# Narrow products for unit 1 as well, and one ScalarE copy for both groups of a half, in a fused embedding, interaction and MLP kernel

## The reference

```python
e = jnp.stack([tbl_f[ids[:, f]] for f in range(32)], axis=1)      # (512, 32, 64)
def layer(X, prev, W, b):
    x = jnp.einsum('bmd,bhd->bmhd', X, prev).reshape(bsz, m * h, d)
    return jnp.einsum('oc,bcd->bod', W, x) + b[None, :, None]
x1 = layer(e, e, W0, b0)          # 128 outputs
x2 = layer(e, x1, W1, b1)         # 128 outputs
z = concat([x1.sum(2), x2.sum(2)], 1)
h = relu(concat([z, dense_ctx], 1) @ W_top1 + b_top1)   # 272 -> 512
h = relu(h @ W_top2 + b_top2)                           # 512 -> 256
y = h @ W_top3                                          # 256 -> 1
```

## Time and profile before

| what | value |
|---|---|
| time, median of 3 runs | 196.35 us (196.08 to 196.5) |
| profiled execution, span from first to last instruction | 194.2 us |
| median less span | 2.15 us |
| TensorE matmul busy | 181.0 us, 93% |
| ScalarE busy | 144.9 us, 75% |
| VectorE busy | 137.3 us, 71% |
| GpSimd busy | 123.8 us, 64% |
| mean granted TensorE clock | 0.991 |

### The profile page before, as it was taken

How to read it: one execution, slowest core, us unless ns; L and a number is a source line. 1 busy time by engine, 2 the same in 40 slices (tenths; PEclk the granted TensorE clock), 3 DMA queues, 4 the chain that set the end, 5 groups by cost and what they waited for, 6 DMA issues and landing times.

```text
span 194.2 us, 8803 instructions
## 1 busy us (share of the span) xinstructions
PE 181.0 (93%) x3815; PEld 157.7 (81%) x3815; DVE 137.3 (71%) x307; ACT 144.9 (75%) x349; POOL 123.8 (64%) x134
## 2 busy tenths in 40 slices
PE   6999999869669959999999999989999999999985
PEld 6999999749557738878898877868888879889984
DVE  2007799994499999999996499977765796693100
ACT  2499977549848997899868879979677797776333
POOL 3777787877777777777777777777777777000000
PEclk9999999999999997999999999999999999999999
DMA  6991111111123334427211411331141114010100
GB/s 182 311 339 33 27 29 24 29 25 30 27 51 64 84 83 75 118 54 177 50 30 30 81 30 30 50 58 30 32 83 32 30 32 75 17 23 14 29 3 0
DMA packets 16520, 12.26 MB, mean 63 GB/s; under 512 B 12513, under 2 KB 12897, under 8 KB 16482
## 3 DMA queue, kind: packets, MB, share of 16 engines
q1 hardware_dynamic: 12242, 7.44, 15.1%
q0 software_dynamic: 4096, 4.20, 11.2%
q10 hardware_dynamic: 144, 0.07, 0.1%
HBM read 9.59 MB, written 0.00 MB: 49 GB/s over the span
## 4 chain that ended last, share of the span: by engine, by line
POOL 47%; PE 31%; issue 16%; DMA 3%; ACT 2%; DVE 0%; ACTq 0%
POOL rows L626 47%; PE psum L458 13%; PE psum L220 7%; PE psum L545 3%; PE psum L527 3%; DMA rows<-table,idx 2%; PE psum L480 2%; PE psum L516 2%; PE psum L190 1%; DMA t_sb<-ids 1%; ACT t_sb L261 1%; PE psum L562 1%; DVE acc_sb L465 0%; ACT acc_sb L731 0%; ACT xx L271 0%
## 5 line engine op out<-in xcount | busy, mean ns | idle before, releaser
L626 POOL DMA_INDIRECT rows<-table,idx x128 | 123.1, 962 | 40.8 <-issue 38.7
L288 DVE TENSOR_TENSOR prod<-psum,xx 128x256 f32<-128x256 f32 (+3 forms) x160 | 85.7, 603 | 22.2 <-ACT xx L271 12.0
L261 ACT ACTIVATE t_sb<-psum 64x308 f32<-64x308 f32 (+1 forms) x180 | 76.4, 425 | 10.2 <-PE psum L205 3.9
L458 PE MATMUL psum<-coef,t_sb 128*64 128x128 f32 (+1 forms) x954 | 53.7, 275 | 0.0
L458 PEld LDWEIGHTS psum<-coef,t_sb 128*64 128x64 f32 (+1 forms) x954 | 47.4, 131 | 4.3 <-issue 4.1
L220 PE MATMUL psum<-prod,xx 64*32 64x154 f32 x1920 | 42.4, 300 | 2.0 <-ACT coef L731 0.9
L257 DVE COPY t_sb<-psum 64x308 f32<-64x308 f32 x64 | 30.8, 481 | 10.8 <-PE psum L220 9.5
L220 PEld LDWEIGHTS psum<-prod,xx 64*32 64x32 f32 x1920 | 30.7, 107 | 9.4 <-issue 5.9
L271 ACT ACTIVATE xx<-psum 128x256 f32<-128x256 f32 x32 | 12.3, 386 | 11.0 <-PE psum L190 10.6
L190 PE MATMUL psum<-ident,rows 128*128 128x128 f32 x64 | 13.6, 295 | 3.1 <-DVE prod L288 2.0
L358 DVE TENSOR_TENSOR t_sb<-t_sb,coef 128x64 f32<-128x64 f32 (+8 forms) x63 | 15.8, 321 | 0.2
(11 more groups left out here) (39 smaller groups left out, 120.9 us busy)
## 6 DMA issues: line engine op xcount, KB each, us to landing
rows<-table,idx POOLq DMA_INDIRECT x128, 2.7
t_sb<-t_sb SPq DMA_DIRECT2D x28, 64.0 KB
w_sb<-w1t SPq DMA_DIRECT2D x3, 512.0 KB, 6.9
t_sb<-w0x SPq DMA_DIRECT2D x1, 768.0 KB, 10.3
w0g_sb<-w0g SPq DMA_DIRECT2D x1, 512.0 KB, 9.2
w_sb<-top SPq DMA_DIRECT2D x2, 256.0 KB
w_sb<-top SPq DMA_DIRECT2D x1, 512.0 KB
w_sb<-w1t SPq DMA_DIRECT2D x1, 384.0 KB, 4.7
```

Of the source, the lines that this page charges most:

```text
L261: copy_t(act, lambda o, i: act.activation(o, i, ACT.Copy), 0, u, v)
L288: return dve.tensor_tensor(at(p, col, out), at(psum, XT[g] * BANK + a, first), at(x, x0 + b, second), ALU.mult)
L458: return pe.matmul(bank(ACC, half * O, O, j, width), t_sb[:, c:c + width], w, start=i < places, stop=i >= n - places, tile_position=(0, j))
L626: pool.indirect_dma_start(rows[:, c:c + D], None, table[:, :], bass.IndirectOffsetOnAxis(ap=idx[:, g:g + 1], axis=0))\
```

## The change

`NARROW` becomes 2, so unit 1 is in narrow form too, and its groups come, with unit 0's, before the coefficient transposes; the row transposes of unit 2's second half lie between the two. `COPIER` alternates between ScalarE and VectorE over the 14 groups. VectorE's products of unit 1's second half move from after the folds to before the far folds. From unit 2 on, VectorE copies p = 1 of the second group as before, and ScalarE copies p = 1 of the first group with two instructions of 64 x 308 and p = 0 of both groups with two instructions of 64 x 616. In unit 15's first half ScalarE copies all four parts with four of the latter form, in its second half ScalarE and VectorE take one p each. For this a half's 16 rows lie differently in T, and `ids` is transposed to match. TensorE waits for copies once for each wide half, for all groups before it.

```diff
-NARROW = 1
+NARROW = 2
...
-        COPIER = [int(n >= 5 and n % 3 == 2) for n in range(V_GROUPS)]
+        COPIER = [n % 2 for n in range(V_GROUPS)]
...
-        def copier(group, p):
-            return int(p == 1 and (group % 2 == 1 if 8 <= group < 4 * (ALL - 1) else group < 8 or group % 4 > 1))
+        BOTH, FIRST_GROUP, SECOND_GROUP = (0, 2), (0, 1), (1, 1)
+        LAST_HALF = 2 * ALL - 1
+
+        def copier(half, n):
+
+            if half < 2 * NARROW or half == LAST_HALF - 1:
+                return [(0, BOTH), (1, BOTH)] if n == 0 else []
+            if half == LAST_HALF:
+                return [(n, BOTH)]
+            return [(1, FIRST_GROUP), (0, BOTH)] if n == 0 else [(1, SECOND_GROUP)]
...
-            for n in range(2):
-                wait(pe, t_copied[n], copied(n, 4 * u + v - 1))
+            for n in range(2 if u < NARROW or v % 2 == 0 else 0):
+                wait(pe, t_copied[n], copied(n, 4 * u + v - (1 if u < NARROW else 0)))
...
+        def wide_copy(eng, copy, n, u, g):
+
+            mine = copier(2 * u + g, n)
+            if not mine:
+                return
+            if u == UNITS and g == 0:
+                eng.wait_ge(coef_tr, V_GROUPS)
+            if u >= 2 * UNITS:
+                eng.wait_ge(block_done, (u - 2 * UNITS) // 2 + 1)
+            for p, (t, groups) in mine:
+                eng.wait_ge(t_done, 4 * u + 2 * g + t + groups)
+                for e in range(2):
+                    src = at(psum, (TG + 2 * t) * BANK + e * COLS, [[1, COLS], [BANK, 2 * groups], [2 * COLS, 2]], D * p, D)
+                    dst = at(t_sb, t_at(u) + g * SUB + GROUP * p + 4 * t, [[CHUNK, COLS], [2, 2 * groups], [1, 2]], D * e, D)
+                    last = copy(dst, src)
+            last.then_inc(t_copied[n], 1)
...
-            for v in range(4):
-                t_group(pe, 0, v)
+            for u in range(NARROW):
+                t_half(pe, u, 0)
+                t_half(pe, u, 1)
+            transpose_rows(pe, 2, 1)
             for n in range(V_GROUPS):
...
-                if n == 10:
-                    transpose_rows(pe, 2, 1)
...
-            t_half(pe, 1, 0)
-            t_half(pe, 1, 1)
...
+            for u in range(NARROW):
+                copies(u, 0)
+                copies(u, 1)
+                fields_in(2, u)
             for n in range(V_GROUPS):
                 if COPIER[n] == 0:
                     copy_coef(act, plain, n)
-                if n == 10:
-                    act_xx(act, 2, 0)
-                    act_gram(act, 2, 0)
...
-            act_xx(act, 2, 1)
-            copies(1, 0)
-            act_gram(act, 2, 1)
-            copies(1, 1)
...
             products(dve, 1, 0)
+            products(dve, 1, 1)
             copied_w(dve, 2)
...
-            products(dve, 1, 1)
...
-            for v in range(4):
-                dve_copy_t(dve, 1, v)
             products(dve, 2, 0)
...
-        a["ids"][NARROW * UNIT:].reshape(-1, TILES // 2, 2, 2, 2, M).transpose(2, 4, 5, 0, 1, 3).reshape(128, -1)], axis=1)
+        a["ids"][NARROW * UNIT:].reshape(-1, 2, 2, 2, 2, 2, M).transpose(2, 5, 6, 0, 1, 3, 4).reshape(128, -1)], axis=1)
```

More of the change, by code:

```diff
@@ L175, in t_at @@
             return u // UNITS % 2 * COLS * CHUNK + u % UNITS * UNIT
-        def copier(group, p):
-            return int(p == 1 and (group % 2 == 1 if 8 <= group < 4 * (ALL - 1) else group < 8 or group % 4 > 1))
+        BOTH, FIRST_GROUP, SECOND_GROUP = (0, 2), (0, 1), (1, 1)
[6 more added lines that the diff above has]
+            return [(1, FIRST_GROUP), (0, BOTH)] if n == 0 else [(1, SECOND_GROUP)]
         def copied(n, groups):
-            return sum(copier(i, p) == n if i // 4 >= NARROW else p == n == 0 for i in range(groups) for p in range(2))
+            halves = sum(copier(h, n) != [] for h in range(2 * NARROW, groups // 2))
+            return (min(groups, 4 * NARROW) if n == 0 else 0) + halves
         def transpose_rows(pe, u, g):
@@ L245, in copy_t, with act_copy_t, dve_copy_t @@
                 eng.wait_ge(block_done, (u - 2 * UNITS) // 2 + 1)
-            eng.wait_ge(t_done, 4 * u + v + 1)
-            if u < NARROW:
[L248 to L264, removed]
+            for p, (t, groups) in mine:
[5 more added lines that the diff above has]
+            last.then_inc(t_copied[n], 1)
+        def act_copy_t(act, u, g):
+            if u < NARROW:
+                narrow_copy(act, u, 2 * g)
+                narrow_copy(act, u, 2 * g + 1)
+            else:
+                wide_copy(act, lambda o, i: act.activation(o, i, ACT.Copy), 0, u, g)
+        def dve_copy_t(dve, u, g):
+            wide_copy(dve, dve.tensor_copy, 1, u, g)
         def act_xx(act, u, g):
@@ L746, in _, with copies, fields_in @@
                 copy_cross(act, n)
-            for g in range(2):
-                act_copy_t(act, 0, 2 * g)
-                act_copy_t(act, 0, 2 * g + 1)
+            def copies(u, g):
+                act_copy_t(act, u, g)
+            def fields_in(u, g):
+                act_xx(act, u, g)
+                act_gram(act, u, g)
+            for u in range(NARROW):
+                copies(u, 0)
+                copies(u, 1)
+                fields_in(2, u)
             for n in range(V_GROUPS):
@@ L886, in _ @@
                 for g in range(2):
-                    dve_copy_t(dve, u, 2 * g + 1)
+                    dve_copy_t(dve, u, g)
                     products(dve, u + 1, g)
             copy_acc(dve, dve.tensor_copy, 7)
-            dve_copy_t(dve, ALL - 1, 2)
-            dve_copy_t(dve, ALL - 1, 3)
+            dve_copy_t(dve, ALL - 1, 0)
+            dve_copy_t(dve, ALL - 1, 1)
             copy_acc(dve, dve.tensor_copy, 8)
```

15 lines of the change are left out of this document (6 added, 9 removed).

## The result

The change made the kernel slower: 199.48 us in the median of 6 runs (197.98 to 200.09) against 196.48 for the kernel before (6 runs, 196.08 to 198.08), a ratio of 1.0142 with a 95% interval of 1.0107 to 1.0176. The forecast was 196.05 with a range of 195.5 to 196.65. The profiled execution took 198.76 us and spans 196.9, 2.7 more than before's 194.2.

What follows compares the result with a forecast made beforehand. GpSimd's row gathers were taken to bound the kernel up to the border near 128 us, TensorE after it. Setup gain 0, merged copies 0.31 us: 194.2 - 0.31 = 193.9, plus 2.15 gives 196.05 us, range 195.5 to 196.65.

Steps and rivals of the forecast that it cites:

- The border: Unit 11's second half, 128.09 us: TensorE waits 0.92 us for gathered rows; only gains after 133 us move the end.
- The setup's sum: First narrow matmuls to first contraction: 16.8 us against 18.07, with one idle gap of 1.52 us kept (bounds 0 to 3.0).
- The conclusion from the bounds: Setup 2.8 us earlier to 0.2 later lies inside TensorE's 0.92 us border wait, so its gain at the end is 0.
- The coarser wait: Wide halves wait for all copies of the half before: hidden by gather wait before 128 us, 0.2 us to spare behind.
- The merged copies: ScalarE's copies take 2.23 us a half, 0.38 less; sum of block 5 at 157.02 us starts 0.31 us earlier.
- The last half's copies: Unit 15's second half: VectorE's two copies take 1.58 us; packing up to 0.25 us later, cost taken as 0.
- What lies around the span: Time outside the profiled span, 2.15 us (median 196.35 against span 194.2), added to the forecast span.
- the merge saves nothing: Rival: merged copies take 0.87 us each, unit 11's first half starts 0.2 us late; 196.55 us, chance 0.06.
- the gathers move: Rival: moved folds shift VectorE-GpSimd meetings; 196.65 us if later (chance 0.13), 195.45 if earlier (0.19 together with rows sooner).
- the setup's gain passes through: Rival: the border is no floor, so 1.3 + 0.31 us less; 194.75 us, chance 0.06.
- rows land sooner: Rival: gathered rows land 0.3 us sooner at the border; 195.75 us, chance 0.19 together with gathers earlier.
- The clock rival: Rival: longer waits for rows drop the clock at 128 us, 1.0 us more; 197.05 us, chance 0.04.

Runs made afterwards that it cites:

- The spread kernels: Kernels with unit 1's narrow groups dealt between the coefficient transposes (e3, e5, e7, e9, e12); ratios to the kernel before 0.9978 to 1.0007.
- e7: e3 with two already satisfied waits in front of the second wide group of every half; ratio to the kernel before 1.0007.
- e9: e3 with 28 already satisfied waits in the setup, before unit 0's narrow groups; ratio to the kernel before 0.9985.
- e11: Changed kernel with the copies, waits and ids of the kernel before for units 2 to 11, merged copies from unit 12 on; ratio to the kernel before 1.0042.
- e5: e1 with unit 1's narrow groups dealt between the coefficient transposes, copies of the kernel before; ratio to the kernel before 0.9978.
- e1: Kernel before with the new setup order alone, old wide copies and waits; median 197.66 us, 0.44% slower than the kernel before.
- e13: e2 with unit 1 copied in the small pieces of the kernel before, merged copies from unit 2 on; ratio to the kernel before 1.0023.
- e12: e3 with merged copies from unit 12 on only; ratio to the kernel before 0.9988.
- e2: Changed kernel with the setup of the kernel before (unit 1 wide, behind the coefficient transposes); 198.81 us.
- e3: Changed kernel with unit 1's narrow groups dealt between the coefficient transposes, ScalarE's copies and transposes' banks to match; ratio to the kernel before 0.9989.
- e4: Changed kernel with 60 one-column matmuls added at the start; ratio 1.1204.
- e10: Changed kernel with every narrow matmul streaming its 77 columns twice; single execution, 14.3 us from first narrow matmul to coefficient transposes.

## Why the prediction was wrong, point by point

*The border* was read rightly: the gathers keep their pace (last one at 164.5 us) and what is won ahead of them is not seen at the end. The spread kernels, up to 0.6 us early at unit 3, gained nothing that can be measured. But the border is not a fixed time. In e7 and e9 TensorE takes the same rows at 127.51 and 127.37 us without a wait, in e11 and e5 it waits until 128.52 and 128.69; the 0.92 us that the prediction counted on is what one execution showed.

*The setup's sum* failed in one term, "I keep that once and put 0 to 3.0 as its bounds". The gap is no single event of 1.52 us: it came after each 256 instructions or so of dense small matmuls, 4.64 us. With it the sum is 8.1 + 0.24 + 4.64 + 0.3 + 6.05 + 0.6 = 19.9 us, and 37.88 + 19.9 = 57.8 agrees with the measured 57.69. Two units have twice the records of one, so a gap per 256 instructions would have given two more from the earlier trace rows alone; the row was read as a single accident.

The Trainium skill, "Runtime: NRT & Kernel Launch", section "Instruction fetch mechanics", was read too narrowly there. Its block of 256 instructions agrees with the spacing of these gaps; its "mostly hidden" does not hold in this stretch, where each block cost 1.42 to 1.63 us.

*The conclusion from the bounds*, that either end lies inside the 0.92 us of waiting, failed with them. The first contraction was 1.84 us late, outside the 0.2 that I had allowed. Even so e1 shows that such a setup alone would have cost 0.4% and not 1.4%.

*The coarser wait* is the second step that failed: "the gather wait hides it before 128 us". I priced it only behind the border, where it costs nothing, as forecast: from 130 to 172 us no wide group waits for a copy. It costs 1.40 us by 107 us when the setup is on time (e13) and 1.26 more than e1 when it is late (2.95 against 1.69). It was to be hidden by the same slack that the setup was to use: the two were each compared with the border's wait, and never added. That slack is about 1.0 us in the changed kernel (2.95 at 107 us, 1.94 at the border); e1, without the coarser waits on the way to the border, took up 1.6.

*The merged copies* were right in mechanism and size: 2.24 for 2.23 us a half, 0.28 for 0.31 us at the sum of block 5. *The last half's copies* cost ScalarE 1.37 and VectorE 1.62 us (forecast 1.58), also right; the wait for packed rows in the tail, 0.69 us in the profiled execution, lies above the bound of 0.25, for a cause that was not in the forecast.

*What lies around the span* was put at 2.15 us from a median and another execution's span; in the changed kernel's profiled execution it is 198.76 - 196.9 = 1.86 us. The size is small beside the loss.

*The rivals:* that the merge saves nothing fell. That the gathers move fell as well in the changed kernel: the slowest took 1.790 us instead of 1.607, and the last started at 164.5 (in e9 it started at 163.5, so they can move). That the setup's gain passes through, or that rows land sooner, could not be tried there, since TensorE came after the rows; in e5 and e12, where the setup was early, the gain went into the wait at the border. The clock rival had the wrong place: it fell not after 128 us but at 75.5. Before the change it had fallen ahead of the border too, at 72.3 and for about as long; what that does to the loss is said below.

## What to carry to other kernels

When two edits draw on the same slack, add their losses ahead of it before comparing with it, and ask of every wait that is made coarser what it costs in the stretch that is said to hide it. A gap without a cause that appears once in a dense run of small matmuls should be expected again in proportion to the instructions; dealing such runs between longer instructions left one gap and at most a short second one here instead of three. A merged copy saves time by itself (0.68 us instead of 0.87 here), but the engine that waits for it waits for the last piece.

## What the runs showed of the hardware that was not expected

Windows of the changed kernel (us; busy TensorE, weight loads, VectorE, ScalarE, GpSimd; granted clock, DMA share, GB/s):

```profile
72.00:75.50 3.50, 1.60 (x71) 1.11 (x54) 3.42 (x8) 3.38 (x8) 2.83 (x3) 1.00 0.41 102
75.50:78.50 3.00, 3.00 (x60) 2.38 (x45) 2.96 (x7) 1.99 (x5) 2.11 (x3) 0.50 0.60 101
```

After a stretch in which TensorE was busy 1.60 of 3.50 us, the clock is at 0.50, the lower level of 1.2 GHz, for some 3 us. The kernel before has the same at 72.5 us, and e1 at 75 us; e11 had none, though its TensorE had stood idle 1.95 us there as in e1. From the row transposes at 73.7 to 73.9 us to the next ones e1 took 5.87 us and e11 4.24, with the same copies: the stretch costs about 1.6 us. That makes the clock a third draw on the same slack. In the kernel before, executions with a mean clock of 1.00 and those with 0.99 take the same time (196.75 and 196.94, 196.26 and 196.27, 196.68 and 196.69 us in the means of three rounds). In the changed kernel, which has no slack left, the one run with a mean clock of 1.00 took 197.98 us, the five at 0.983 or 0.991 took 198.76 to 200.09, 199.53 in the mean. So I estimate that some 1.5 us of the loss come only together with the lower clock and as much comes without it; one run at 1.00 is few for that.

The lower clock can come behind the stops of the setup as well: in e2 at 55 us, after waits of 1.97 and 1.85 us, and in e3 at 44 us, after the gap of 2.03. In the changed kernel's profiled execution it did not come there, after gaps of 1.63, 1.42 and 1.59 us.

One-column matmuls are no cheap filler: 120 records of them took 22.5 us in e4, 0.19 us each, most of them at the lower level: the granted clock was 0.50 from 10 to 34 us, where the kernel before stands at 1.00.

Doubling the columns of a narrow matmul from 77 to 154 lengthened a run of 128 from 2.13 to 2.60 us, a fifth (one execution, e10): most of a narrow matmul's time here does not go with its columns.
